# Router and expert projections of a routed attention layer in one unrolled block

## The chip, the cores and the metric

The program runs on one core of a Trainium2 chip. Its time is the device time of that core in microseconds (us): from the first to the last instruction, with a little around them. Five engines work in parallel, each through its own list of instructions in order: TensorE (PE, matrix products; PEld are its weight loads), VectorE (DVE), ScalarE (ACT), GpSimd (POOL) and SyncE (SP, which here only issues DMAs). They wait for one another by semaphores. DMAs are issued from SP, ACT or POOL and run on 16 shared DMA engines.

## The reference

A stack of four layers over 2048 tokens of 128 channels. The change touches one sublayer, the routed attention of layer 2 (`l2f_` in names):

```python
h = relu(layer_norm(x @ rW1.T + rb1, eps=1e-5) * ln_g + ln_b)
probs = softmax(h @ rW2.T + rb2)                  # 8 experts
tp, ti = top_k(probs, 2); tp = tp / tp.sum()
for e in range(8):                                # each expert is an attention with weights of its own
    q, k, v = heads(x @ qW[e].T + qb[e]), heads(x @ kW[e].T + kb[e]), heads(x @ vW[e].T + vb[e])
    out += ((softmax(q @ k.T * scale) @ v) @ oW[e].T + ob[e]) * gate[e]
```

Here x is the normalised input; there are 16 heads of 8 channels. Keys and values are needed of all tokens for all experts, queries only of the tokens that chose the expert.

## The kernel before

The sublayer `l2_ffn` has four stages, each a block (all engines meet at a block's end):

- `l2_router` (L2046): normalises the tokens (`NormBlock`: DVE statistics, PE transposes, ACT copies to `channels_n`), makes the hidden layer (PE L2118, DVE L2179 to L2189), logits (PE L2129), top 2 (DVE), each token's slot in a list sorted by expert (DVE L2214 to L2246), and adds the output bias (PE L2147). It also fills constants: POOL sets `v_and_ones` to one, and SP copies rows of ones into the two buffers of `k_parts` (L255, four DMAs of 96 KB that end in 3 partitions each).
- `l2_prepare` (L2252): a hardware loop of four rounds with two experts in each. Per expert, PE transposes four weight matrices (L2360), projects keys for all tokens into four PSUM banks (L161) and values in two halves (L2367, L2427). Keys are kept as three bf16 parts: ACT writes part hi (L2400), DVE the rest (L2422), ACT part mid (L2402), DVE part lo (L2431). SP stores everything in DRAM: `expert_w_out_dram`, `expert_w_q_dram`, `expert_v_dram` (L2312), then six DMAs of `l2f_k_parts_dram` (L281). Part buffers are double (`part_`, `other_`), the buffer of values is single, and so SP's stores of values must land before DVE writes the next (`v_stored`). SP also loads the weights (L2293) and biases (L2298 to L2302) of the expert after next, behind the stores of this one in its queue; the biases of keys and queries come as columns, 4 bytes to a partition. Beside it POOL scatters 32 times 128 token numbers into `query_list_dram` (L2344), loads two lines of that list (L2019) and gathers the tokens of the first two query tiles (L2023).
- `attention_loop` (starts with DVE L994) and `l2_collect`: not touched.

The order in each engine is as written; nothing reorders it.

Of the kernel before, what the change touches and what calls it, by code (L numbers as in the profile page):

```python
# [22 lines left out]
F32 = mybir.dt.float32  # L23
# [207 lines left out]
class AttentionConstants:  # L231
# [17 lines left out]
    def sync(self, sp):  # L249
        self.wait(sp)  # L250
        at = self.at
        ones = at.ones[:, :].unsqueeze(1).to_broadcast([3, NPAIR, T])
        for k in range(self.buffers):
            for j in range(2):
                sp.dma_start(at.kx[64 * j + ROWS:64 * j + ROWS + 3, k, :, :], ones).then_inc(self.ones_set, 16)  # L255
# [18 lines left out]


def store_keys(at, eng, e, parts, parts_ready, count, parts_stored):
    eng.wait_ge(parts_ready, count)
    for which, part in enumerate(parts):
        n = len(range(NR)[ROWS_OF_K[which]])
        for j in range(2):  # L280
            eng.dma_start(at.k_dram[bass.ds(e, 1), j, :, :, ROWS_OF_K[which], :].rearrange("e p d n t -> (e p d) n t"),  # L281
                          part[64 * j:64 * j + 64, :].unsqueeze(1).to_broadcast([64, n, T])).then_inc(parts_stored, 16)
# [1744 lines left out]
def l2_ffn(c, at, ins, fixed):  # L2027

    c.layer = "l2f_"
    E, K = 8, 2
    with ExitStack() as ctx:
        rt = Routed(c, ctx, E, K)
        gate = c.sb(ctx, "gate", [P, K, NT], F32)
        slot = c.sb(ctx, "slot", [P, K, NT], mybir.dt.uint32)
        row = c.sb(ctx, "row", [P, NT], mybir.dt.uint32)
        y_row = c.sb(ctx, "y_row", [P, K, NT], mybir.dt.uint32)
        l2_router(c, ins, rt, E, K, gate, slot, row, y_row, fixed)  # L2040
        l2_prepare(c, at, ins, rt, slot, row)
        attention_loop(c, at, 3, routed=rt)
        l2_collect(c, rt, gate, y_row)


def l2_router(c, ins, rt, E, K, gate, slot, row, y_row, fixed):  # L2046

    nc, ps = c.nc, c.ps
    W = P // 2
    with ExitStack() as ctx:  # L2050
# [4 lines left out]
        h, hh = c.sb(ctx, "hidden", [P, NT, W], F32), c.sb(ctx, "hidden_squared", [P, NT, W], F32)  # L2055
        hT = c.sb(ctx, "hiddenT", [W, T], F32)
# [6 lines left out]
        counts, offset = c.sb(ctx, "tile_counts", [P, NT, E], F32), c.sb(ctx, "tile_offset", [P, NT, E], F32)  # L2063
        more, tiles_of = c.sb(ctx, "more", [P, E, NT], F32), c.sb(ctx, "tiles_of", [P, E], F32)
        first, end, index = c.sb(ctx, "first_tile", [P, E], F32), c.sb(ctx, "end_tile", [P, E], F32), c.sb(ctx, "partition", [P, 1], F32)
# [3 lines left out]
        mixT = c.sb(ctx, "mixT", [E, T], F32)  # L2069
        norm = NormBlock(c)  # L2070
        (w_loaded, drawn, chain, wT_psum, wT_ready, h_psum, hvar_ready, hstd_ready, h_ready, hT_psum, hT_ready, lg_psum, shifted, exp_ready,
         sel_ready, rank_psum, mix_ready, mixT_psum, mixT_ready, ranked, of_tile_ready, of_tile_psum, ob_psum) = (c.sem("r_" + n) for n in (
             "w_loaded", "drawn", "chain", "wT_psum", "wT_ready", "h_psum", "hvar_ready", "hstd_ready", "h_ready", "hT_psum", "hT_ready",
             "lg_psum", "shifted", "exp_ready", "sel_ready", "rank_psum", "mix_ready", "mixT_psum", "mixT_ready", "ranked", "of_tile_ready",
             "of_tile_psum", "ob_psum"))
        loads = [(w1[:, :], ins["L2_ffn_rW1"]), (w2[:, :], ins["L2_ffn_rW2"]), (ob[:, :], ins["L2_ffn_ob"]),
                 (b1[:, :], row_view(ins["L2_ffn_rb1"], W)), (g1[:, :], column(ins["L2_ffn_ln_g"])),
                 (g0[:, :], column(ins["L2_ffn_ln_b"])), (b2[:, :], row_view(ins["L2_ffn_rb2"], E))]
# [8 lines left out]
        with nc.Block() as block:  # L2087
            @block.sync
            def _(sp):
                for dst, src in loads:  # L2090
                    sp.dma_start(dst, src).then_inc(w_loaded, 16)
                fixed.sync(sp)
                fixed.sync_end(sp)

            @block.gpsimd
            def _(pool):
                draw_order(c, pool, order, E, drawn)
# [3 lines left out]
                nc.gpsimd.memset(before[:, :], 1.0).then_inc(drawn, 1)  # L2101
                pool.wait_ge(drawn, DRAWN - 1)
# [3 lines left out]
                fixed.gpsimd()  # L2106
                fixed.wait(pool)

            @block.tensor
            def _(pe):  # L2110
                pe.wait_ge(w_loaded, 16 * len(loads))
                nc.tensor.transpose(ps[:, 4, 0:W], w1[:, :], c.ident[0:W, 0:W])
                nc.tensor.transpose(ps[0:W, 4, W:W + E], w2[:, :], c.ident[0:E, 0:E]).then_inc(wT_psum, 1)
                norm.tensor(pe)
                pe.wait_ge(wT_ready, 2)
                pe.wait_ge(norm.nT_ready, NC)
                for t in range(NT):
                    ins_ = nc.tensor.matmul(ps[:, 4 + t // 8, (t % 8) * W:(t % 8 + 1) * W], c.nT[:, t * P:(t + 1) * P], w1T[:, :],  # L2118
                                            start=True, stop=True)
                    if t % 8 == 7:  # L2120
                        ins_.then_inc(h_psum, 1)
                pe.wait_ge(h_ready, 1)
                for t in range(NT):
                    ins_ = nc.tensor.transpose(ps[0:W, t // 4, (t % 4) * P:(t % 4 + 1) * P], h[:, t, :], c.ident[:, :])
                    if t % 4 == 3:
                        ins_.then_inc(hT_psum, 1)
                pe.wait_ge(hT_ready, NC)
                for t in range(NT):
                    last = nc.tensor.matmul(ps[:, 6, t * E:(t + 1) * E], hT[:, t * P:(t + 1) * P], w2T[:, :], start=True, stop=True)  # L2129
                last.then_inc(lg_psum, 1)  # L2130
                pe.wait_ge(drawn, DRAWN)
                pe.wait_ge(sel_ready, 1)
                chosen = sel[:, :, :].rearrange("p t e -> p (t e)")
                nc.tensor.matmul(ps[:, 7, 0:P], before[:, :], chosen, start=True, stop=True)
                nc.tensor.matmul(ps[:, 7, P:2 * P], ones[:, :], chosen, start=True, stop=True)
                nc.tensor.matmul(ps[:, 7, 2 * P:2 * P + 1], before[:, :], ones[:, 0:1], start=True, stop=True).then_inc(rank_psum, 1)
                pe.wait_ge(mix_ready, 1)
                for t in range(NT):
                    ins_ = nc.tensor.transpose(ps[0:E, t // 4, (t % 4) * P:(t % 4 + 1) * P], mix[:, t, :], c.ident[:, :])
                    if t % 4 == 3:  # L2140
                        ins_.then_inc(mixT_psum, 1)
                pe.wait_ge(of_tile_ready, 1)
                nc.tensor.transpose(ps[0:1, 6, 0:P], of_tile[:, :], c.ident[:, :]).then_inc(of_tile_psum, 1)
                pe.wait_ge(mixT_ready, NC)
# [674 lines left out]
```

## Time and profile before

| | us |
|---|---|
| median of three runs | 3931.2 (3928.16 to 3935.24) |
| the profiled execution | 3919.58 |
| its span, first to last instruction | 3917.9 |
| `l2_router` in it | 1998.6 to 2067.6 |
| `l2_prepare` in it | 2068.0 to 2278.2 |
| attention of the sublayer starts | 2278.2 |

Times in the rows below are us from the start of the span. In a timeline row the first number is the start, the second the duration; "x" is the number of instructions merged; in brackets is the idle time before and what ended it. In a row of stretches, each engine has its busy time and its number of instructions; PEclk is the granted clock of TensorE (1.00 is 2.4 GHz, 0.50 is 1.2 GHz), then come the busy share of the DMA engines and the GB/s moved.

### The profile page before, as it was taken

The page shows a single profiled execution, that of the slowest core. Times are in us where ns is not written, and L with a number is a line of the kernel's source. Part 1 is how long each engine was busy: PE and PEld are TensorE (multiplying, and loading weights), DVE is VectorE, ACT ScalarE, POOL GpSimd, SP SyncE. Part 2 cuts the span into 40 slices and gives each one's busy share as a digit, 9 for nine tenths or more (in the row PEclk, how much of TensorE's full clock was granted, in tenths as well). Part 3 has the DMA queues.
Part 4 walks back from the last instruction along what each step waited for, and adds up shares of the span by engine and source line. Part 5 has one row for each costly group of instructions (what it writes and reads, how often), then busy time and mean ns, then how long its engine had stood idle before and what let it go on. Part 6 is the DMA issues. An engine that isn't in the chain of part 4 may idle for free. (4 is left out here: it accounts for less than half of the span.)

```text
span 3917.9 us, 127868 instructions
## 1 busy us (share of the span) xinstructions
PE 3201.4 (82%) x54200; PEld 2084.5 (53%) x54200; DVE 2926.3 (75%) x3610; ACT 2528.6 (65%) x4873; POOL 601.5 (15%) x1574
## 2 busy tenths in 40 slices
PE   2999999479998897565764449999999999999638
PEld 1666666335555674122433326666666666666424
DVE  5999999458884113898353359999999999999653
ACT  1899999447777333432211229999999999999622
POOL 0010000011100000464004011111111111111220
PEclk7999999779999898899866769999999999999859
DMA  5000000310000000540008755555454545455410
GB/s 117 9 8 9 7 10 5 84 34 11 9 7 3 22 16 9 173 144 31 5 5 129 234 152 123 130 124 134 117 135 117 135 116 135 117 135 117 108 32 11
DMA packets 198682, 295.81 MB, mean 76 GB/s; under 512 B 93668, under 2 KB 128042, under 8 KB 197062
## 3 DMA queue, kind: packets, MB, share of 16 engines
q1 hardware_dynamic: 191478, 276.38, 28.3%
q10 hardware_dynamic: 2048, 6.29, 0.9%
q8 instruction: 423, 6.93, 0.8%
q0 software_dynamic: 4592, 5.05, 0.6%
q14 instruction: 141, 1.16, 0.1%
HBM read 225.51 MB, written 53.39 MB: 71 GB/s over the span
## 5 line engine op out<-in xcount | busy, mean ns | idle before, releaser
L890 ACT ACTIVATE channels_qk<-psum 128x512 f32<-128x512 f32 x3842 | 2061.1, 595 | 263.7 <-PE psum L716 189.6
L958 DVE TENSOR_REDUCE l2f_chunk_max<-psum 128x2 f32<-128x1024 f32 x1144 | 1324.8, 1217 | 76.3 <-PE psum L691 67.8
L958 DVE TENSOR_REDUCE chunk_max<-psum 128x2 f32<-128x1024 f32 (+2 forms) x832 | 916.8, 1156 | 112.2 <-PE psum L691 62.6
L691 PE MATMUL psum<-l2f_k_parts,l2f_q_parts 48*128 48x512 bf16 x2288 | 697.0, 388 | 42.5 <-DVE l2f_chunk_max L958 31.2
L737 PE MATMUL psum<-channels_qk,l2f_v_and_ones 128*9 128x128 f32 x17920 | 698.5, 274 | 14.1 <-issue 14.1
L716 PE MATMUL psum<-l2f_q_parts,l2f_k_parts 51*128 51x128 bf16 x8968 | 706.5, 218 | 0.4 <-ACT l2f_minus_max_rows L938 0.4
L691 PE MATMUL psum<-k_parts,q_parts 48*128 48x512 bf16 (+3 forms) x1664 | 424.5, 382 | 103.2 <-DMA q_parts<-q_rows_dram 73.6
L716 PEld LDWEIGHTS psum<-l2f_q_parts,l2f_k_parts 51*128 51x128 bf16 x8968 | 482.4, 94 | 30.7 <-ACT channels_qk L890 23.2
L737 PE MATMUL psum<-channels_qk,v_and_ones 128*9 128x128 f32 x12544 | 492.7, 275 | 0.6 <-ACT channels_qk L890 0.5
L716 PE MATMUL psum<-q_parts,k_parts 51*128 51x128 bf16 x6272 | 432.5, 218 | 31.1 <-DMA q_parts<-minus_max_rows 10.5
L737 PEld LDWEIGHTS psum<-channels_qk,l2f_v_and_ones 128*9 128x9 f32 x17920 | 386.0, 90 | 121.3 <-issue 23.7
L691 PEld LDWEIGHTS psum<-l2f_k_parts,l2f_q_parts 48*128 48x128 bf16 x2288 | 208.5, 94 | 296.0 <-issue 157.5
L716 PEld LDWEIGHTS psum<-q_parts,k_parts 51*128 51x128 bf16 x6272 | 288.4, 94 | 93.8 <-ACT channels_qk L890 56.2
L737 PEld LDWEIGHTS psum<-channels_qk,v_and_ones 128*9 128x9 f32 x12544 | 271.0, 90 | 77.6 <-issue 11.2
L691 PEld LDWEIGHTS psum<-k_parts,q_parts 48*128 48x128 bf16 x1664 | 122.3, 94 | 288.0 <-issue 145.6
L1714 PE MATMUL psum<-l1a_state_c,identity 128*128 128x512 f32 x256 | 125.7, 616 | 89.4 <-DVE l1a_state_c L1699 89.4
L1413 DVE SCALAR_TENSOR_TENSOR x_normalised<-psum,l0f_expert_weights,x_normalised 128x128 f32<-128x128 f32 x128 | 36.0, 344 | 196.4 <-PE psum L1377 196.4
L609 POOL TENSOR_TENSOR l2f_minus_max_parts<-l2f_minus_max,l2f_one 128x4 bf16<-128x4 f32 x143 | 28.4, 199 | 916.6 <-DVE l2f_minus_max L965 916.6
L1665 ACT ACTIVATE psum<-l1a_delta,l1a_a 128x1024 f32<-128x1024 f32 x64 | 71.5, 1118 | 147.0 <-DVE l1a_input L1694 147.0
L1398 ACT ACTIVATE l0f_hidden<-psum,l0f_b_now 128x512 f32<-128x512 f32 x128 | 87.9, 687 | 118.2 <-PE psum L1368 118.2
L609 POOL TENSOR_TENSOR minus_max_parts<-minus_max,one 128x4 bf16<-128x4 f32 x128 | 25.5, 199 | 902.3 <-DVE minus_max L965 902.3
L1714 PEld LDWEIGHTS psum<-l1a_state_c,identity 128*128 128x128 f32 x256 | 43.9, 189 | 171.2 <-DVE l1a_state_c L1699 137.4
(476 smaller groups left out, 3178.0 us busy)
## 6 DMA issues: line engine op xcount, KB each, us to landing
l2f_k_parts<-l2f_k_parts_dram SPq DMA_DIRECT2D x588, 192.0 KB, 3.8
l2f_v_and_ones<-expert_v_dram SPq DMA_DIRECT2D x144, 288.0 KB, 4.3
l1a_bc_rows<-ssm_rows_dram SPq DMA_DIRECT2D x32, 512.0 KB, 4.7
expert_v_dram<-l2f_v_and_ones SPq DMA_DIRECT2D x8, 1152.0 KB, 4.3
channels_qk<-ssm_rows_dram SPq DMA_DIRECT2D x16, 512.0 KB
l2f_q_parts<-l2f_gathered_q_parts SPq DMA_DIRECT2D x444, 16.0 KB
k_parts<-k_rows_dram ACTq DMA_DIRECT2D x32, 192.0 KB, 7.6
q_parts<-q_rows_dram SPq DMA_DIRECT2D x64, 96.0 KB, 2.5
```

Of the source, the lines that this page charges most:

```text
L609: return g_.tensor_tensor(dst, src, ones.to_broadcast(list(src.shape)), ALU.mult)
L691: last = nc.tensor.matmul(c.ps[:, 2 * (n % 2) + j, 0:width], at.q[64 * j:64 * j + ROWS, tile % SLOTS, pair, :], kx(tile)[64 * j:64 * j + R ...
L716: last = nc.tensor.matmul(c.ps[:, ring.bank(i, place[j]), (2 * kk + pp) * P:(2 * kk + pp + 1) * P], kx(i)[64 * j:64 * j + ROWS + 3, pair, ...
L737: last = nc.tensor.matmul(oT[32 * m:32 * m + HD + 1, g * P:(g + 1) * P], vx(i)[:, kt, 4 * g + m, :], at.prob[:, s % 4, j, kk, pp * P:(pp + ...
L890: nc.scalar.activation(at.prob[:, s % 4, j, 0:kts, :].rearrange("p k q -> p (k q)"), c.ps[:, ring.bank(i, n), 0:kts * 2 * P], ACT.Exp, sca ...
L958: v.tensor_reduce(at.mx[:, 4 * g + 2 * pp:4 * g + 2 * pp + 2, chunk], c.ps[:, 2 * (n % 2):2 * (n % 2) + 2, 0:span.width(tile, chunk)], X, ...
L1398: nc.scalar.activation(mid[:, k % 2, f, :], ps[:, f, :], ACT.Gelu, bias=bnow[:, k // NC, f:f + 1]).then_inc(gelu_done, 1)
L1413: last = v.scalar_tensor_tensor(c.n[:, tile, :], ps[:, 4 + k % 2, t * P:(t + 1) * P], mix[:, tile, bass.ds(r * 2 + e, 1)], c.n[:, tile, :] ...
L1665: nc.scalar.activation(decay(step), delta[:, h, tokens(step)], ACT.Exp, scale=a[:, h, n:n + 1]).then_inc(da_ready, 1)
L1714: last = nc.tensor.matmul(ps[:, 2 * (step % 2) + b, :], c.ident[:, :], hc[:, step % U, b * 512:(b + 1) * 512], start=False, stop=step % S ...
```

## The change

`l2_router` and `l2_prepare` become one function, `l2_front`, with one block and no loop. Its parts:

- All weights are loaded at its start: expert 0's by four DMAs, the other seven's by four DMAs of 7 x 64 KB, into the second buffer of `k_parts`, which is free until the attention; all value biases by one DMA. Biases of keys and queries come as rows (two DMAs of 8 x 128), are reordered by ACT and transposed by PE.
- The router's loads are issued from ACT, not SP.
- The values have both buffers of `v_and_ones`, in quarters over two PSUM banks.
- Each engine's list holds an expert's steps and the router's in turn; the router's PSUM is bank 7 alone, so its transposes and logits take turns with ACT bank by bank.
- POOL makes part lo of experts 0 to 3, DVE of 4 to 7. The scatter on POOL comes after these, when DVE has the slots.
- The ones of `k_parts`' second buffer are placed at the end, when the weights there are no longer read.

```diff
             @block.sync
             def _(sp):
-                for dst, src in loads:
-                    sp.dma_start(dst, src).then_inc(w_loaded, 16)
-                fixed.sync(sp)
+                for n, m in enumerate("qkvo"):
+                    sp.dma_start(w[:, 0, n, :], ins[f"L2_ffn_{m}W"][0]).then_inc(w_loaded, 16)
...
+                    sp.dma_start(w[:, 1:E, n, :], ins[f"L2_ffn_{m}W"][1:E].rearrange("e p d -> p e d")).then_inc(all_w_loaded, 16)
...
+                fixed.place(sp, 0)
+                sp.wait_ge(norm.n_ready, NC)
+                sp.dma_start(rt.n_dram[:, :].rearrange("(t p) d -> p t d", p=P), c.n[:, :, :]).then_inc(n_stored, 16)
+                sp.wait_ge(rw_ready, 4)
+                for e in range(E):
+                    store_expert(e)
+                sp.wait_ge(o_stored, 32 * E)
+                fixed.place(sp, 1)
                 fixed.sync_end(sp)
...
+                def store_expert(e):
+                    sp.wait_ge(hi_ready, 4 * e + 4)
+                    store_part(e, 0)
+                    sp.wait_ge(wT_ready, 3 * e + 3)
+                    sp.dma_start(rt.w_out_dram[e], wT[:, e, 2, :]).then_inc(o_stored, 16)
+                    sp.dma_start(rt.w_q_dram[e], w_q[:, e, :]).then_inc(o_stored, 16)
+                    sp.wait_ge(v_ready, QUARTERS * (e + 1))
...
+                    sp.wait_ge(mid_ready, e + 1)
+                    store_part(e, 1)
+                    sp.wait_ge(lo_ready, e + 1)
+                    store_part(e, 2)
...
             @block.gpsimd
...
+                for e in range(E // 2):
+                    pool.wait_ge(rest_ready, 4 * e + 4)
+                    pool.wait_ge(mid_ready, e + 1)
+                    nc.gpsimd.tensor_tensor(parts[e % 2][2][:, :], rest, parts[e % 2][1][:, :], ALU.subtract).then_inc(lo_ready, 1)
                 pool.wait_ge(scattered, 16)
+                pool.wait_ge(slots_ready, 1)
...
             @block.scalar
+                def keys_hi(e):
+                    if e >= 2:
+                        act.wait_ge(parts_stored[e % 2], 96 * (e // 2))
                     for n in range(NC):
-                        act.wait_ge(k_psum, e * 4 + (n + 1))
+                        act.wait_ge(k_psum, 4 * e + n + 1)
...
             @block.vector
+                def values(e, quarters):
+                    if e >= 2:
+                        dve.wait_ge(v_stored[e % 2], 16 * (e // 2))
...
+                keys_rest(3)
...
+                link(v.tensor_copy(ranks[:, :], ps[:, 7, 0:2 * P + 1]))
+                values(3, range(QUARTERS))
...
+                keys_rest(4)
...
+                v.memset(many[:, 0:1], float(rt.least // 2)).then_inc(slots_ready, 1)
```

**PE**, from the normalised tokens on. Before, the router's products stand alone, and the loop with the experts' begins behind a branch; `l2f_w_qkvo` are the weights.

```order
L153 MATMUL psum<-identity,x_normalised 128x128 x16
L2118 MATMUL psum<-l2f_rw1T,channels_n 128x64 x16
L2124 MATMUL psum<-identity,l2f_hidden 64x128 x16
L2129 MATMUL psum<-l2f_rw2T,l2f_hiddenT 128x8 x16
L2134 MATMUL psum<-l2f_selected,l2f_before 128x128
```

Now (`l2f_k_parts` is the buffer in which the weights and their transposes lie, `channels_qk` the one in which the hidden layer lies):

```order
L153 MATMUL psum<-identity,x_normalised 128x128 x16
L2192 MATMUL psum<-identity,l2f_k_parts 128x128 x4
L161 MATMUL psum<-channels_n,l2f_k_parts 128x512 x4
L2214 MATMUL psum<-l2f_rw1T,channels_n 128x64 x16
L2207 MATMUL psum<-l2f_k_parts,channels_n 128x128 x16
L2192 MATMUL psum<-identity,l2f_k_parts 128x128 x4
L161 MATMUL psum<-channels_n,l2f_k_parts 128x512 x4
L2221 MATMUL psum<-identity,channels_qk 64x128 x16
L2207 MATMUL psum<-l2f_k_parts,channels_n 128x128 x16
L2192 MATMUL psum<-identity,l2f_k_parts 128x128 x4
L2265 MATMUL psum<-l2f_rw2T,channels_qk 128x8 x16
L161 MATMUL psum<-channels_n,l2f_k_parts 128x512 x4
```

The keys of expert 0 now stand ahead of the hidden layer, and the logits (L2265) behind the values of expert 1.

**SP**, one expert's steps. Before, the row of six key stores (L281, the first of them shown) stands between loads of weights ahead and of biases behind; ISA rows are waits on counts that a register holds.

```order
L2293 DMA l2f_w_qkvo<-in_L_ffn_oW_dram 128x128
L2308 ISA
L2308 DMA expert_w_out_dram<-l2f_wT_qkvo 128x128
L2309 ISA
L2310 ISA
L2310 DMA expert_w_q_dram<-l2f_w_and_b_q 128x129
L2311 ISA
L2312 ISA
L2312 DMA expert_v_dram<-l2f_v_and_ones 128x2304
L281 ISA
L281 DMA l2f_k_parts_dram<-l2f_part_hi 64x3x2048
```

Now, from the last loads to the first step of expert 1:

```order
L2127 DMA l2f_k_parts<-in_L_ffn_vb_dram 128x1024
L257 DMA l2f_k_parts<-l2f_ones_rows 3x8x2048 x2
L2131 DMA normalised_tokens_dram<-x_normalised 128x16x128
L2104 DMA l2f_k_parts_dram<-l2f_part_hi 64x3x2048 x2
L2111 DMA expert_w_out_dram<-l2f_k_parts 128x128
L2112 DMA expert_w_q_dram<-l2f_w_and_b_q 128x129
L2114 DMA expert_v_dram<-l2f_v_and_ones 128x2304
L2104 DMA l2f_k_parts_dram<-l2f_part_mid 64x2x2048 x2
L2104 DMA l2f_k_parts_dram<-l2f_part_lo 64x2048 x2
L2104 DMA l2f_k_parts_dram<-l2f_other_hi 64x3x2048 x2
```

No load stands between two experts' stores any more, and part hi goes out ahead of the values.

## Rows read from the trace of the kernel before

**Rows 1.** Stretches: the two blocks. Start:end, length, engines, PEclk, DMA share, GB/s.

```profile
1998.00:2068.00 70.00, 34.59 (x153) 29.80 (x153) 38.85 (x143) 11.39 (x19) 7.11 (x30) 0.52 0.04 7
2068.00:2278.00 210.00, 83.56 (x356) 60.60 (x356) 59.48 (x63) 40.81 (x67) 40.06 (x41) 0.67 0.83 194
```

**Rows 2.** Timeline: last copy to channels_n; first instruction of prepare; first of attention.

```profile
2012.43 0.60 ACT L177 ACTIVATE channels_n<-psum 128x512 f32<-128x512 f32 x1 [0.43 <-PE psum L153]
...
2068.03 0.33 SPq L2293 DMA_DIRECT2D l2f_w_qkvo<-in_L_ffn_qW_dram  x1
...
2278.18 0.48 DVE L994 MEMSET psum<- 128x512 f32 x1 [27.05 <-PEq L2280]
```

**Rows 3.** Waits, 2066 to 2300: waiter and releaser, us in total, times, longest.

```profile
ACT l2f_part_hi L2400 <- DMA l2f_w_and_b_q<-in_L_ffn_qb_dram: 68.4, 3, 37.5
...
ACT l2f_other_hi L2400 <- DMA l2f_w_and_b_q<-in_L_ffn_qb_dram: 39.9, 4, 15.0
...
DVE l2f_v_and_ones L2427 <- DMA expert_v_dram<-l2f_v_and_ones: 33.6, 6, 17.2
```

**Rows 4.** Timeline of SP: stores of values, experts 5 and 6.

```profile
2216.64 0.33 SPq L2312 DMA_DIRECT2D expert_v_dram<-l2f_v_and_ones  x1
...
2238.17 0.33 SPq L2312 DMA_DIRECT2D expert_v_dram<-l2f_v_and_ones  x1
```

**Rows 5.** DMA issues, 1980 to 2330: KB each, us from issue to landing.

```profile
expert_v_dram<-l2f_v_and_ones SPq DMA_DIRECT2D x8, 1152.0 KB, 4.3
l2f_k_parts_dram<-l2f_part_hi SPq DMA_DIRECT2D x8, 768.0 KB, 10.0
```

**Rows 6.** Stretches: ones placed; two under the scatter; one expert's stores; the first load.

```profile
2008.00:2024.00 16.00, 11.25 (x48) 9.76 (x48) 7.43 (x19) 2.39 (x4) 0.00 (x0) 0.50 0.15 24
2100.00:2110.00 10.00, 0.18 (x1) 0.18 (x2) 1.23 (x1) 0.00 (x0) 7.60 (x8) 0.50 1.05 79
...
2120.00:2130.00 10.00, 0.00 (x0) 0.00 (x0) 0.00 (x0) 0.00 (x0) 0.00 (x0) 0.62 1.05 98
2238.00:2254.00 16.00, 4.90 (x20) 4.20 (x20) 5.76 (x5) 2.61 (x5) 0.00 (x0) 0.50 0.92 275
...
4.00:6.00 2.00, 0.00 (x0) 0.00 (x0) 0.00 (x0) 0.00 (x0) 0.00 (x0) 1.00 1.04 323
```

**Rows 7.** Timeline of PE: keys of an expert; half of its values at either clock.

```profile
2084.90 3.60 PE L161 MATMUL psum<-channels_n,l2f_wT_qkvo 128*128 128x512 f32 x8
...
2088.33 1.95 PE L2367 MATMUL psum<-l2f_wT_qkvo,channels_n 128*128 128x128 f32 x16
...
2243.89 3.78 PE L2367 MATMUL psum<-l2f_wT_qkvo,channels_n 128*128 128x128 f32 x16 [4.64 <-DVE l2f_v_and_ones L2427]
```

**Rows 8.** Groups by line in the router, 1998 to 2068: busy, mean ns, idle before.

```profile
L2118 PE MATMUL psum<-l2f_rw1T,channels_n 128*128 128x64 f32 x32 | 7.1, 422 | 0.8 <-ACT channels_n L177 0.8
L2129 PE MATMUL psum<-l2f_rw2T,l2f_hiddenT 64*128 64x8 f32 x32 | 7.0, 358 | 0.9 <-ACT l2f_hiddenT L2163 0.9
...
L2124 PE MATMUL psum<-identity,l2f_hidden 128*64 128x128 f32 x16 | 3.6, 421 | 8.2 <-DVE l2f_hidden L2189 8.2
```

**Rows 9.** Timeline of DVE in the router: first and last of the slots' chain.

```profile
2048.37 0.07 DVE L2216 MEMSET l2f_tile_offset<- 128x8 f32 x1
...
2059.05 0.17 DVE L2246 TENSOR_SCALAR l2f_y_row<-l2f_where 128x16 uint32<-128x16 f32 x1
```

**Rows 10.** Timeline of POOL: first scatter; list loaded; tokens gathered.

```profile
2074.05 1.05 POOL L2344 DMA_INDIRECT query_list_dram<-l2f_row,l2f_slot  x1 [3.16 <-DMA query_list_dram<-l2f_blank_list]
...
2135.60 1.17 POOL L2019 DMA_DIRECT2D l2f_gathered_index<-query_list_dram  x2 [17.69 <-DMA query_list_dram<-l2f_row,l2f_slot]
...
2144.56 0.97 POOL L2023 DMA_INDIRECT l2f_gathered_tokens<-normalised_tokens_dram,l2f_gathered_index  x1 [0.31 <-issue]
```

**Rows 11.** DMA queue of POOL in 2090 to 2100 and in 2120 to 2130: packets, MB, share.

```profile
q0 software_dynamic: 53, 0.00, 0.4%
...
q0 software_dynamic: 242, 0.00, 5.1%
```

More of the change, by code:

```diff
@@ L2079, in l2_router @@
+        ROUTER_LOADS = 16 * len(router_loads)
         DRAWN = E + NT + 3
@@ L2105, in _ @@
                                         pattern=[[1, P]], channel_multiplier=-1).then_inc(drawn, 1)
[L2106 to L2144, printed above, removed]
-                pe.wait_ge(ranked, 1)
-                for t in range(NT):
-                    ins_ = nc.tensor.matmul(ps[:, 4 + t // 4, (t % 4) * P:(t % 4 + 1) * P], mixT[:, t * P:(t + 1) * P], ob[:, :],
-                                            start=True, stop=True)
-                    if t % 4 == 3:
-                        ins_.then_inc(ob_psum, 1)
@@ new lines, in _ @@
+                turn_weights(0)
+                pe.wait_ge(rw_loaded, ROUTER_LOADS)
+                nc.tensor.transpose(ps[:, 7, 0:W], w1[:, :], c.ident[0:W, 0:W])
+                nc.tensor.transpose(ps[0:W, 7, W:W + E], w2[:, :], c.ident[0:E, 0:E])
+                pe.wait_ge(b_ordered, 2)
+                for n in range(2):
+                    last = nc.tensor.transpose(ps[:, 7, P + n * E:P + (n + 1) * E], b_order[:, n, :], c.ident[0:E, 0:E])
+                last.then_inc(rw_psum, 1)
+                norm.tensor(pe)
@@ new lines, in _ @@
+                turn_weights(1)
+                pe.wait_ge(norm.nT_ready, NC)
+                project_keys(0)
+                pe.wait_ge(rw_ready, 4)
+                project_hidden(0)
+                pe.wait_ge(h_added, 1)
+                project_hidden(1)
+                project_values(0, range(QUARTERS))
+                turn_weights(2)
+                project_keys(1)
+                pe.wait_ge(h_ready, 1)
+                for k in range(NC):
+                    turn_hidden(k)
+                project_values(1, range(QUARTERS))
@@ new lines, in _ @@
+                turn_weights(3)
+                pe.wait_ge(hT_ready, NC)
+                for t in range(NT):
+                    last = nc.tensor.matmul(ps[:, 7, t * E:(t + 1) * E], hT[:, t * P:(t + 1) * P], w2T[:, :], start=True, stop=True)
+                last.then_inc(lg_psum, 1)
+                project_keys(2)
+                project_values(2, range(QUARTERS))
+                turn_weights(4)
+                project_keys(3)
+                pe.wait_ge(drawn, DRAWN)
+                pe.wait_ge(sel_ready, 1)
@@ new lines, in _ @@
+                evacuate(c, act, 0, c.nT, norm.nT_psum, 0, norm.nT_ready)
+                copy_weights(1)
+                act.wait_ge(rw_ready, 4)
+                keys_hi(0)
+                keys_mid(0)
+                act.wait_ge(hvar_ready, 1)
+                nc.scalar.activation(total[:, :], total[:, :], ACT.Sqrt).then_inc(hstd_ready, 1)
+                copy_weights(2)
+                keys_hi(1)
+                for k in range(NC):
+                    act.wait_ge(hT_psum, k + 1)
+                    nc.scalar.activation(hT[:, k * 512:(k + 1) * 512], ps[0:W, 7, :], ACT.Relu, bias=g0[:, :], scale=g1[:, :]).then_inc(hT_ready, 1)
@@ L2409, in _ @@
+                for k in range(NC):
+                    act.wait_ge(mixT_psum, k + 1)
+                    nc.scalar.activation(mixT[:, k * 512:(k + 1) * 512], ps[0:E, 7, :], ACT.Copy).then_inc(mixT_ready, 1)
+                keys_mid(5)
+                copy_weights(7)
+                for e in (6, 7):
+                    keys_hi(e)
+                    keys_mid(e)
             @block.vector
@@ L2411, in _ @@
                 v = nc.vector
[L2412 to L2418 removed]
+                link = Chain(dve, chain)
@@ L2436, in l2_collect @@
+                keys_rest(7)
+                values(7, range(QUARTERS))
+                keys_lo(7)
 def l2_collect(c, rt, gate, y_row):
```

504 lines of the change are left out of this document (265 added, 239 removed).

## The prediction

> **What bounds the kernel now.** The change touches two blocks, so I read the stretches of these first, then the marks of their ends, then who waits in them, and last the DMA queues. The two blocks take from 1998.6 to 2278.2, 280 us of the 3917.9 [rows 1, 2]. In the first, the DMA engines are busy 4% of the time, and neither PE (34.6 us of 70) nor DVE (38.9) is full: the router is one dependent chain. In the second they are busy 83% of 210 us and move 194 GB/s, while PE has 83.6 us of work, DVE 59.5, ACT 40.8 [rows 1]. So the second block is the DMA queue's: it waits for data only a sixth of its time, the first leaves it idle.
>
> Two things keep the queue from doing better. First, a loop between stores and loads: the biases of expert e+2 are issued behind the stores of e, and ACT, which opens an expert's keys, waited 68.4 + 39.9 us for them; DVE waited 33.6 us for the single buffer of values [rows 3]. From one store of values to the next it takes 21.5 us [rows 4], of which the queue is full for 16, from 2238 to 2254 [rows 6]. Second, the scatter. It began at 2074 and had landed at 2135.6 [rows 10]. Under it the queue shows a share of 1.05 and yet moves 79 and 98 GB/s; without it, 275 [rows 6].
>
> **What must be moved.** Per expert 1152 KB of values [rows 5], keys of 2 x 768 KB for part hi [rows 5], and in the same shape (3, 2 and 1 rows of the six) 2 x 512 and 2 x 256 for mid and lo, with some 128 KB of weights: 4352 KB or 4.46 MB. At 275 GB/s that is 16.2 us, for eight experts 130 us. The change moves the same.
>
> **The change, part by part.**
>
> *Loads first.* 2.1 MB of weights, 0.5 MB of value biases: the nearest row is the load of the kernel's start, 323 GB/s [rows 6], so 8 us; twice that if pieces of 512 bytes in seven experts at once go slower. It lies beside the normalisation, which ends at 2013.0 [rows 2], and costs nothing at either end. The column loads of biases and the weight loads between stores go: with them goes the wait of rows 3.
>
> *Keys of expert 0 ahead of the router.* From 2013.0, PE transposes and projects, ACT copies, DVE makes the rest: I put the first store at 2021 (transposes and their copies 2, keys 6, all at the low clock). The store of normalised tokens, 1 MB, goes ahead of it and is done by then.
>
> *Experts 0 to 3 and the router in one order.* PE per expert: keys 3.6 us at clock 1.00 [rows 7], 7.2 at 0.50; values 2 x 1.95 or 2 x 3.78 [rows 7]; transposes about 1. That is 8 or 16 us. Between them stand hidden layer 7.1, its transposes 3.6, logits 7.0 [rows 8] and the small products for the ranks, say 1.5, all at the low clock. To the values of expert 3 this is 4 x 16 + 19 = 83 us at the low clock and about 42 at the high; PE also waits for DVE's layer norm of the hidden layer (8.2 us before [rows 8], part of it now under values; I take 6) and, bank 7 being one, four times for ACT between transposes (4 us). So the values of expert 3 are ready at 2013 + 93 = 2106 on a low clock. On a high one the queue leads instead: 2021 + 4 x 16.2 = 2086. PE granted 0.67 over the old block [rows 1] and will be fuller here: I take the middle, 2096. Values, mid and lo of expert 3 then need another 10 us: half the stores are out at **2106** (2096 to 2115). The queue has gaps in this part, because part hi goes out early and then SP stands at `v_ready` until DVE has worked off the router's piece ahead of the values; behind it in SP's list are mid and lo, and nothing else waits for them as the buffers are double.
>
> *The scatter.* It needs DVE's slots: behind the values of expert 3 stand the chain of slots, 10.8 us from L2216 to L2246 [rows 9], and the rest of expert 4, 3 us of DVE's 7.4 per expert (59.5 over 8, [rows 1]), less a count of about 1 us that is put off. So it starts at 2096 + 12.5, about 2109. POOL's own part lo of experts 0 to 3 is long done. It took 61.5 us before [rows 10]; I take that. With it go 61.5 x 0.088 = 5.4 MB of stores, at the mean of 79 and 98 GB/s [rows 6]. It ends at 2170; list and gather end 10 us later [rows 10] and are hidden by the stores.
>
> *Stores of experts 4 to 7.* 17.8 MB from 2106 on: 0.8 until 2109, 5.4 under the scatter, 11.6 behind it at 275 GB/s, 42 us: to 2212. The compute of an expert (PE at most 16 us; DVE 7.4 and ACT 5.1, an eighth of rows 1) hides under 16.2 us of stores, with double buffers. The old scatter phase had other small transfers in it; if the queue does better there, this term falls by up to 15 us, and if large stores hold the scatter up to 80 us it grows by 12.
>
> *Ones at the end.* Two of the four copies of ones are now behind the last store. The four took 16 us at 24 GB/s, 2008 to 2024 [rows 6], as they end in three partitions; two take **8 us**, uncovered.
>
> *The attention* begins at 2212 + 8 = 2220 instead of 2278.2: **58 us** earlier; one block boundary less gives half a us. Nothing behind it changes.
>
> The sum: 3919.6 - 59 = 3860.6 for an execution like the profiled one. The median of the runs shown lies 11.6 above that execution, so I predict 3931.2 - 59 = **3872**. Ends of the terms, fast clock and quick scatter: 2096 + 3 + 50, 5.1 MB moved under it, 11.9 MB at 299 GB/s (275 over its share 0.92) to 2189, + 8 = 2197, gain 81. Slow: 2115 + 3 + 75, 10.4 MB left, 38, + 8 = 2239, gain 39.
>
> A rule of the skill bears on the scatter's term. The row shows the scatter's queue at 5.1% of the engines [rows 11] while the stores fall to a third. The Trainium skill, DMA: Bandwidth & Descriptors, Queues, rings and completion order, says that each engine takes turns between queues packet by packet; a packet of 4 bytes should then cost a store packet almost nothing. By that rule the stores would run on at 260 under the scatter; it is rival A. The same page, Specifications, says that writes under 512 bytes are read-modify-write, which speaks for the row.
>
> **Rivals.**
>
> A. *The scatter was not what slowed the queue.* The stretch 2080 to 2130 also held column loads, and its share is over 1 with little moved; what slowed it may go with the change. Then all 17.8 MB run at 275 GB/s from 2106: 65 us, to 2171, + 8 = 2179: gain 99, **3832**. For it: the small share [rows 11]. Against: the columns came with every expert, and the stretches with them but without a scatter are fast [rows 6].
>
> B. *The experts run in lockstep all the same.* Engines take their lists in order; if each expert's chain (copy, rest, mid, lo, then the stores) lies open as before, each costs 21.5 us [rows 4], and hidden layer and logits, 14 us of PE [rows 8], lie open between the first four. Half the stores are then out at 2021 + 86 + 14 = 2121; 3 + 61.5 us of scatter bring 1.4 experts, the other 2.6 take 56, and 8: to 2249, gain 29, **3902**. For it: PE at the low clock needs 16 us an expert, no less than the stores. Against: the bias loads that closed the loop are gone. That the order on paper does nothing, because the router's pieces wait for one another anyway, ends in the same place.
>
> C. *Slower than before: the scatter starves.* In 2090 to 2100 it got 53 packets, against 242 in 2120 to 2130 [rows 11], while POOL issued at the same pace. At the mean of the two, 148, its 61.5 us hold about 910. If large stores hold it at 53 per 10 us throughout, it lasts 171 us from 2109, and list and gather follow: 2290, so that the attention starts 12 us late, **3943**. It decides from a scatter of 159 us on. Against: with large key stores beside it (2120 to 2130) it ran at its best pace.
>
> **How the numbers follow.** My case (gain 39 to 81) 0.64; A (81 to 105) 0.15; B (5 to 39) 0.16; C 0.03; no change 0.02. The range leaves out about half of A and most of B and all of C: gain 36 to 91, so 3840 to 3895. A measurement of this kernel can tell about 0.2%, 8 us, from no change. Faster by more: 0.64 + 0.15 + 0.15 = 0.94; within 0.02 + 0.01; slower 0.03.
>
> **What the profile of the changed kernel would show.** The first key store at 2020 to 2025 (loads and early keys). Waits of ACT's keys on a DMA of biases gone; in their place waits of ACT for its part buffer in experts 4 to 7, when the queue leads. Stores of values of experts 0 to 3 spaced by 17 to 21 us with a queue that is not full; a scatter starting at 2105 to 2115 and lasting 50 to 75 us with 80 to 100 GB/s beside it; 16 us an expert at a full queue behind it; and 8 us of 24 GB/s at the very end. It would be wrong if the scatter let the stores pass (A), if the queue kept gaps after 2170 (B), or if the gather ended the block (C). Outside the block times must stay as they are.

## The result, and the profile after

The changed kernel takes 3840.1 us (median of 4 runs, 3830.1 to 3844.4), the kernel before 3930.6 (3928.2 to 3935.2): a ratio of 0.976, with an interval of 0.975 to 0.978. That is 90 us less where 59 were forecast: the median lies on the range's lower end, and the ratio on the 3931.2 us that the forecast started from gives 3838, below it. The profiled execution took 3844.4 with a span of 3842.6, its block of router and experts 198.4 us (1994.52 to 2192.94) where the two blocks had 279.6 [rows 2].

The first fence is SP's timeline of the block (start, length, instruction), the second POOL's, the third DVE's: first load; first store of keys; values and the last keys of expert 3; the last step before the values of expert 5 and these; the last keys of expert 7; the ones; first scatter and the load of the finished list; the attention's first instruction.

```profile
1994.52 0.33 SPq L2122 DMA_DIRECT2D l2f_k_parts<-in_L_ffn_qW_dram  x1
...
2013.58 2.76 SPq L2104 DMA_DIRECT2D l2f_k_parts_dram<-l2f_part_hi  x2
...
2082.22 1.72 SPq L2114 DMA_DIRECT2D expert_v_dram<-l2f_v_and_ones  x1
...
2086.09 4.92 SPq L2104 DMA_DIRECT2D l2f_k_parts_dram<-l2f_other_lo  x2
...
2110.57 0.45 SPq L2112 DMA_DIRECT2D expert_w_q_dram<-l2f_w_and_b_q  x1
2142.34 0.33 SPq L2114 DMA_DIRECT2D expert_v_dram<-l2f_v_and_ones  x1
...
2177.04 4.92 SPq L2104 DMA_DIRECT2D l2f_k_parts_dram<-l2f_other_lo  x2
2182.00 2.14 SPq L257 DMA_DIRECT2D l2f_k_parts<-l2f_ones_rows  x2
```

```profile
2091.67 2.43 POOL L2170 DMA_INDIRECT query_list_dram<-l2f_row,l2f_slot  x1 [12.77 <-DVE l2f_many L2479]
...
2147.66 1.17 POOL L2012 DMA_DIRECT2D l2f_gathered_index<-query_list_dram  x2 [13.04 <-DMA query_list_dram<-l2f_row,l2f_slot]
```

```profile
2192.94 0.48 DVE L987 MEMSET psum<- 128x512 f32 x1 [24.82 <-PEq L2098]
```

The stretches of the same profile (start:end, length, PE's granted clock, the DMA engines' busy share, GB/s):

```profile
2020.00:2030.00 10.00, 0.52 0.39 93
2030.00:2040.00 10.00, 0.82 0.91 286
...
2060.00:2070.00 10.00, 0.66 0.51 149
2070.00:2080.00 10.00, 1.00 0.98 277
...
2090.00:2100.00 10.00, 0.66 0.93 256
2100.00:2110.00 10.00, 0.74 1.02 118
...
2130.00:2140.00 10.00, 0.50 0.86 80
...
2150.00:2160.00 10.00, 1.00 0.94 275
2160.00:2170.00 10.00, 0.98 0.94 299
...
2186.00:2188.00 2.00, 0.50 0.18 25
```

They show four parts: from 2013 to 2091 a queue that is full but for two holes (2020, 2060); the scatter, with 118 to 126 GB/s beside it in 2100 to 2130 and 80 in 2130 to 2140; a full queue at 275 to 299; and at the end 25 GB/s of ones. Under the scatter SP also stands at `v_ready` for 31 us (2110.57 to 2142.34), as the values of expert 5 come late; what this does to the block is taken up with the runs without a scatter. The wait of ACT's keys for bias loads [rows 3] is gone. What PE's first pieces cost now, from its timeline (keys of expert 0, hidden layer, logits):

```profile
2008.99 3.78 PE L161 MATMUL psum<-channels_n,l2f_k_parts 128*128 128x512 f32 x8
2012.61 1.89 PE L2214 MATMUL psum<-l2f_rw1T,channels_n 128*128 128x64 f32 x16
2015.35 3.10 PE L2214 MATMUL psum<-l2f_rw1T,channels_n 128*128 128x64 f32 x16 [0.85 <-DVE channels_qk L2400]
...
2045.11 3.73 PE L2265 MATMUL psum<-l2f_rw2T,channels_qk 64*128 64x8 f32 x32
```

Hidden layer (1.9 + 3.1) and logits (3.7) took 8.7 us where they took 14.1 [rows 8]: PE was granted 0.78 in 2013.6 to 2091.0 instead of 0.52 in the old router [rows 1].

### The profile page after: what moved, and what is told of

It is laid out like the page before. It is cut to its first block and busy times, and to the rows that moved or that the text cites. A ratio compares the mean times of both kernels' runs of the same rounds, so it can differ in the third digit from the quotient of the medians.

```text
span 3842.6 us, 127345 instructions
## 1 busy us (share of the span) xinstructions
PE 3198.5 (83%) x54198; PEld 2078.6 (54%) x54198; DVE 2924.8 (76%) x3614; ACT 2528.8 (66%) x4874; POOL 616.8 (16%) x1578
## 5 line engine op out<-in xcount | busy, mean ns | idle before, releaser
L951 DVE TENSOR_REDUCE chunk_max<-psum 128x2 f32<-128x1024 f32 (+2 forms) x832 | 916.5, 1153 | 109.2 <-PE psum L684 61.5
```

The costliest lines, as they stand in the source:

```text
L951: v.tensor_reduce(at.mx[:, 4 * g + 2 * pp:4 * g + 2 * pp + 2, chunk], c.ps[:, 2 * (n % 2):2 * (n % 2) + 2, 0:span.width(tile, chunk)], X, ...
```

## Experiments

The block is counted from the first load to the attention's first instruction, the rest from there to the end of the span. Block and rest are each from one profile of the kernel, times are medians of several executions; "beside" is the kernel before in the same comparison. The same kernel's block differed by up to 11 us between profiles, so smaller differences of block say little. Chips A and B are two chips on which the comparisons ran; the kernel before takes 3930 us on A and 3907 to 3910 on B.

| kernel | chip | block | rest | time | beside | ratio (interval) |
|---|---|---|---|---|---|---|
| before_again | B | 280.7 | 1642 | 3919.6 (one execution) | 3910.5 | |
| before_third | A | 290.5 | 1650 | 3928.5 | 3930.3 | 1.000 (0.998 to 1.001) |
| after_again | B | 192.5 | 1649 | 3835.5 | 3906.5 | 0.981 (0.979 to 0.983) |
| after_third | A | 195.4 | 1650 | 3841.9 | 3930.3 | 0.977 (0.975 to 0.979) |
| before_unrolled | B | 273.8 | 1642 | 3909.9 | 3910.5 | 1.000 (0.999 to 1.001) |
| router_first | A | 248.6 | 1651 | 3892.7 | 3932.7 | 0.990 (0.988 to 0.992) |
| one_v_buffer | A | 201.7 | 1650 | 3842.7 | 3930.3 | 0.977 (0.975 to 0.979) |
| before_no_scatter | A | 255.2 | 1651 | 3894.5 | 3932.7 | 0.990 (0.988 to 0.992) |
| after_no_scatter | A | 171.3 | 1653 | 3812.7 | 3932.7 | 0.970 (0.968 to 0.972) |
| half_scatter | A | 185.2 | 1653 | 3827.3 | 3930.3 | 0.974 (0.972 to 0.976) |
| scatter_paced | B | 232.2 | 1646 | 3869.8 | 3910.5 | 0.989 (0.988 to 0.991) |
| ones_by_row | A | 196.2 | 1655 | 3840.5 | 3932.7 | 0.976 (0.974 to 0.978) |
| ones_early | B | 198.3 | 1643 | 3840.1 | 3910.5 | 0.981 (0.980 to 0.983) |
| ones_in_attention | B | 195.1 | 1650 | 3833.5 | 3906.5 | 0.982 (0.980 to 0.983) |
| parts_first | B | 198.0 | 1640 | 3825.5 | 3906.5 | 0.979 (0.978 to 0.981) |
| both | B | 188.5 | 1653 | 3827.4 | 3906.5 | 0.980 (0.978 to 0.982) |

### What the scatter costs

*after_no_scatter*, *before_no_scatter*: POOL's loop of 32 scatters and the wait for them are out.

```
-                for t in range(NT):
-                    for k in range(K):
-                        nc.gpsimd.indirect_dma_start(out=rt.list_dram...)
-                pool.wait_ge(scattered, 16 * (1 + K * NT))
```

> The changed kernel with the 32 scatters of the list left out; the list stays zero, so every slot names row 0 and the output is another, with the same amount of work behind it. Theory S (the scatter takes the engines' time from the stores): 8.3 MB moved in its 56 us would need 30 us at 275 GB/s, so the block ends 26 us earlier (attention 172 us after the block's start instead of 198) and the time is about 3814; the stalls of PE and DVE in 2100 to 2140, which no data explains, are gone. Rival D (the stores were slow there because their data came late, SP standing at v_ready from 2110.6 to 2142.3): within 8 us of 3840, the same stalls.

> The kernel before with the 32 scatters left out (same remark on the list). Theory S: 61.5 us at 88 instead of 275 GB/s cost 42 us, of which the loop between loads and stores (21.5 us an expert, eight of them 172 of the 210 us) leaves 38 to be seen: 3892. Rival A of the prediction (the scatter is innocent): 3930, and the stretches around 100 us after the block's start still move 80 to 100 GB/s.

3812.7 and 3894.5 where theory S had 3814 and 3892. The block of the changed kernel is 24 to 27 us shorter, that of before 35 on the same chip (290.5 to 255.2). In the stretches of after_no_scatter the place is filled:

```profile
2090.00:2100.00 10.00, 0.82 0.95 297
2100.00:2110.00 10.00, 0.70 0.94 260
```

So the scatter takes the stores' time, and rival A falls: a queue with under a tenth of the share takes over half of the other's bytes. Two ways are open for it: the stores that are queued go slower, or the values come late (SP at `v_ready`) so that fewer are queued. Rival D had the late values as a cause of their own; they are not, since without the scatter SP's 31 us there shrink to at most 4.2. The slower stores alone can cost as much: in after_again (chip B) SP's longest wait for values is 8.2 us, the engines do not stop, the DMA share stays above 1 from 2100 to 2150, and the block is about as long (192.5). From its stretches:

```profile
2110.00:2120.00 10.00, 0.82 1.11 149
...
2140.00:2150.00 10.00, 0.50 1.07 153
```

The rule of turns by packets (the Trainium skill, DMA: Bandwidth & Descriptors, Queues, rings and completion order) does not tell this loss; the measurement decides.

*scatter_paced*: four semaphores in turn, each scatter waits for the fourth before it. *half_scatter*: `for k in range(1)`, the second choice's rows are not scattered.

```
+                        n = K * t + k
+                        if n >= 4:
+                            pool.wait_ge(paced[n % 4], 16 * (n // 4))
```

> The changed kernel with at most 4 scatters on their way at a time instead of about 10. Theory F (a long row of scatter packets in each engine's queue holds up stores and fetches of code): the stops of 5 to 17 us shrink, SP gets its values of expert 5 earlier than 2142, 5 to 10 us gained: 3832. Rival G (each scattered word costs an engine its time, however they are spread): the scatter lasts as long or longer, and the time stays within 4 us of 3840.

> The changed kernel with 16 of the 32 scatters (the second choice's are left out, so the list is incomplete and the output another). Theory T (the stores lose by the time in which a scatter is under way, some 0.45 to 0.55 of their rate): it lasts about 30 us instead of 56 to 60, and the block is 12 to 15 us shorter. Rival N (it is the number of words, each 0.1 us of an engine): the same here, but it would have made scatter_paced cost nothing; only a cost that does not halve (under 6 or over 20 us) speaks against both.

Pacing made it worse, by 34 to 40 us of block; neither F nor G had that. The scatter lasted from 2088.1 to 2213.8. POOL's wait, and two stretches:

```profile
POOL query_list_dram L2174 <- DMA query_list_dram<-l2f_row,l2f_slot: 83.9, 23, 9.5
```

```profile
2130.00:2140.00 10.00, 0.50 0.97 129
2140.00:2150.00 10.00, 0.84 1.13 170
```

In 2100 to 2160 the stores got 129 to 170 GB/s, with four scatters on their way at most. Half the scatters lasted 39 us (2078.8 to 2118.2), not the 30 expected, and cost 14 us of block over none, where all 32 cost 24 in 55.6 us: 0.35 and 0.43 us for each us under way. The paced kernel's block is 61 us longer than without a scatter, but this is not all the stores' loss. From 2210 to 2218 the DMA engines are idle (share 0.00 to 0.01): stores and ones are through at about 2210, 219 us into the block and some 48 us later than the whole block without a scatter, which is 0.39 for each of 122 us. The last 13 us are the scatter's own end, the list and the gather, the path that rival C of the prediction had. The loss goes by time, roughly, and not by the number of words, since the paced kernel scatters as many as the others. The way to make it cheaper is to make it shorter.

### What each part of the change brings

*router_first*: PE, ACT and DVE do the whole router ahead of expert 0; all else as in the changed kernel. PE's list:

```
-                project_keys(0)
                 pe.wait_ge(rw_ready, 4)
                 project_hidden(0)
...
                 for q in range(QUARTERS):
                     add_out_bias(q)
-                    project_values(6, (q,))
...
+                for e in range(E):
+                    project_keys(e)
+                    project_values(e, range(QUARTERS))
```

> The changed kernel with the interleave alone undone: on PE, ACT and DVE all steps of the router stand ahead of all steps of the experts; loads, bias rows, double buffer and unrolled code stay. Theory I (the interleave is worth the time in which the queue stood idle): first key store about 70 us after the block's start instead of 19, then 130 us of stores, 30 us for the scatter, 8 of ones: attention at 238 instead of 198, time about 3880. Rival L (most of the gain is the loop of loads that went; the router's steps only push the experts' steps back when mixed with them, PE being slow): at most 15 us lost, 3855.

The order is worth 53 us of block and 52 of time, more than I had put down: the first store of keys comes at 2073.44, 86 us into the block, and until then the queue stands:

```profile
2030.00:2040.00 10.00, 0.50 0.00 1
```

Part of this is where the scatter stands. DVE has the slots at 2049.82, while the queue is idle, but POOL's list still has the scatter behind part lo of expert 3, so that it starts at 2117.92, beside the stores. A router ahead of the experts with its scatter in the idle stretch was not run; how much of the 53 us it would save is open.

*before_unrolled*: Python loops for `eng.Fori`. *one_v_buffer*: values of all experts go through `at.v[:, 0]`, and DVE waits for the store of those before.

```
-                with eng.Fori(0, E // 2) as r:
+                for r in range(E // 2):
```

```
-                    if e >= 2:
-                        dve.wait_ge(v_stored[e % 2], 16 * (e // 2))
+                    if e >= 1:
+                        dve.wait_ge(v_stored[(e - 1) % 2], 16 * ((e - 1) // 2 + 1))
```

> The kernel before with the loop over the experts written out, nothing else changed. Theory U (unrolling as such brings no time, the gain is in the order and the loads, and costs a little where the scatter runs: code that is not in a loop is fetched by DMA, and the fetches wait behind the scatter, which is what stopped PE, DVE and ACT in 2105 to 2140 of the changed kernel): 3930 to 3945, with waits of DVE or PE of 5 to 17 us for nothing in the trace while the scatter runs. Rival V (the stops come from something else in the changed kernel): no such waits, 3925 to 3932.

> The changed kernel with one buffer of values instead of two: the values of expert e+1 wait until the store of those of e has landed, some 7 us after its issue. Theory B (the double buffer matters little, since part hi of the next expert is stored meanwhile and the old 33.6 us of waits were mostly the scatter's): under 8 us slower than after_third. Rival M (values and stores then run in lockstep, some 4 us for each of eight experts): 30 us slower.

Unrolling brings nothing (1.000; its one profile has a block 7 us shorter than before_again's), the second buffer 1 us of time (6 of block, in one profile each). router_first is still 40 us faster than before. The loads that left the queue are the likely cause, as the experts no longer take 21.5 us each [rows 4], but this is argued by exclusion and not shown: no run puts them back, and part lo on POOL, the biases as rows and part hi ahead of the values were not tried alone either.

### The end of the block

*ones_by_row*: each copy of ones in three, one partition each, in 16 pieces. *ones_early*: the two copies ahead of mid and lo of expert 7. *ones_in_attention*: behind the loads of tile 0, PE waits before tile 1.

```
+            for r in range(3):
+                sp.dma_start(self.at.kx[row:row + 1, k, :, :].rearrange("p a (b t) -> p (a b) t", b=2), ...)
```

```
-                fixed.place(sp, 1)
-                fixed.sync_end(sp)
...
+                routed.fixed.place(sp, 1)
                 for g in range(G - 1):
                     load_group(1, g, second)
```

> The changed kernel with every copy of ones split in three, one partition each in 16 pieces of 2 KB, so that 16 DMA engines share it instead of 3. Theory E (the last 8 to 10 us are three engines' work): the end term falls to 2 us, time about 3833. Rival P (the six receiving partitions set the rate): the same 8 to 10 us, 3840.

> The changed kernel with the last two copies of ones ahead of the stores of parts mid and lo of expert 7 instead of behind them. Theory H (the copies hold 3 of 16 engines, 0.18 of the queue's share, and the six receiving partitions set their pace): the stores run beside them and the 8 us shrink to 2 or 3: 3834. Rival Q (each engine works off its own row of packets, so that the three that carry ones are late with their part of the stores by the same 8 us): 3840.

> The changed kernel with the last two copies of ones issued in the attention's block, behind the loads of tile 0, and waited for by PE ahead of tile 1. Theory Y (the copies at the block's end are uncovered, 8 to 10 us): 8 to 10 us less than after_again. Rival Z (the first tiles' loads are the bound there and the copies push them back): within 3 us of after_again.

None brought time. By row, the copies keep all engines busy and move hardly more than the 25 GB/s of three engines (stretches of ones_by_row): the number of engines does not set the pace, as rival P has it. Whether the six partitions written or the three read do was not separated.

```profile
2176.00:2178.00 2.00, 0.50 0.99 31
2178.00:2180.00 2.00, 0.50 0.97 29
```

ones_early's block is as long as the changed kernel's, as rival Q has it. With the ones in the attention the time is 3833.5 against after_again's 3835.5, as rival Z has it. The attention gives back what it was spared: the ones stand ahead of loads in SP's list, the load of the row maxima is issued 48.3 us after the attention's start (2178.67) instead of 39.4 (after_again, start 2189.11), and PE waits for it. Ahead after_again, then ones_in_attention:

```profile
2234.04 0.69 PE L709 MATMUL psum<-l2f_q_parts,l2f_k_parts 51*128 51x128 bf16 x9 [2.33 <-issue]
```

```profile
2232.13 0.69 PE L712 MATMUL psum<-l2f_q_parts,l2f_k_parts 51*128 51x128 bf16 x9 [10.84 <-issue]
```

The block itself is not shorter in this profile (195.1 against 192.5), since its last keys were stored 7.6 us later than after_again's.

*parts_first*: SP stores mid and lo ahead of the values in experts 0 to 5; *both*: with the ones in the attention.

```
+                    if e >= 6:
+                        store_values()
                     sp.wait_ge(mid_ready, e + 1)
                     store_part(e, 1)
                     sp.wait_ge(lo_ready, e + 1)
                     store_part(e, 2)
+                    if e < 6:
+                        store_values()
```

> The changed kernel with the stores of parts mid and lo ahead of the store of values for experts 0 to 5. In the changed kernel SP stands at v_ready from 2021.2 to 2029.9 and from 2061.0 to 2068.0 while mid and lo (1.5 MB, 5.6 us of queue) of that expert are ready from 2020.5 and 2062.5. Theory W (the block is the sum of bytes over 275 GB/s plus the queue's idle stretches): about 10 us less, block 189. Rival X (what the queue gains in front it gives back at the scatter, or the values then come late and hold the double buffer): within 3 us of after_again.

> The two edits together: W and Y give 18 us less than after_again, X and Z nothing.

The hole closes (263 GB/s in 2020 to 2030 instead of 93), half of the stores are out 2 to 5 us sooner, but the block had 198.0 and 188.5 us against 192.5 to 198.4 without the edit. 3825.5 and 3827.4 against 3835.5 us: the ratio's intervals overlap with after_again's. A few us may be in it; it is not shown, and no version here surely beats the changed kernel.

### The same kernels again, on two chips

> The kernel before, unchanged, for a second profile. Four profiles of variants show 1650 to 1655 us from the start of the attention to the end of the program, the profile of before 1640. Theory J (the profiled execution of before was a fast one behind the block, by chance): about 1651 here and a span of 3929, with 280 us in the two blocks. Rival K (the new code slows the attention): 1640 again.

> The kernel before, unchanged, timed and profiled beside after_third on one chip. If the chips differ in the block of before, the two blocks are not 280 to 281 us here; if they differ in the attention, it takes more than 1642 us.

> The changed kernel, unchanged, beside the next three on one chip, and for a second profile. Block of 198 to 200 us again (84 of gain against the 281 of before); the stops of PE and DVE under the scatter (17.5 and 10.0 us in the first profile, none in the profile of ones_early, whose block had the same length) may or may not be there: if the block keeps its length without them, they cost nothing.

> The changed kernel, unchanged. Block 193 to 199 us, attention 1640 to 1655; the gain in time is that of the two blocks, 82 to 88 us, if nothing outside them differs, and 70 to 75 if the attention gives back some 10.

before_again was to tell whether the new code slows the attention (rival K) or the first profile of before was fast behind the block by chance (J, some 1651 us). It had 1642, which spoke for K; before_third, on A, then had 1650, like the changed kernel there, so on A the new code does not slow the attention. On B the changed kernel had 1649 and its variants 1640 to 1653, and there it is open.

On chip B the gain is 71 us, on A 88. In one profile each, the block of before differs, 280.7 and 290.5, the changed one's hardly (192.5, 195.4). The blocks alone would give 88 us on B and 95 on A; of the 17 and 7 us that are missing in the times, 6 on B lie behind the block (1642 and 1649), the others are not explained by these profiles. On A, before stands still under its scatter. From before_third, timelines of DVE and PE, and a stretch:

```profile
2084.79 1.22 DVE L2427 TENSOR_TENSOR l2f_v_and_ones<-psum,l2f_b_v 128x1024 f32<-128x1024 f32 x1 [18.44 <-issue]
2105.19 1.23 DVE L2427 TENSOR_TENSOR l2f_v_and_ones<-psum,l2f_b_v 128x1024 f32<-128x1024 f32 x1 [19.18 <-remote]
```

```profile
2086.07 3.78 PE L2367 MATMUL psum<-l2f_wT_qkvo,channels_n 128*128 128x128 f32 x16 [19.01 <-issue]
```

```profile
2080.00:2090.00 10.00, 0.50 0.02 0
```

The engines stop for 18 and 19 us while nothing that they need is late in the trace, the stores have nothing to send, and the first keys go out at 2108.78, 125 us into the block and after the scatter (2058.9 to 2106.2). In before_again they left at 2085.09, 90 us into it. The changed kernel has the same stops on A (after_third):

```profile
ACT l2f_k_parts L2303 <- remote: 24.7, 1, 24.7
DVE l2f_v_and_ones L2390 <- remote: 20.8, 3, 9.2
...
DVE l2f_other_lo L2382 <- issue: 9.3, 1, 9.3
```

after_again on B has none, and its block is as long; that half of the stores are out by then and what is queued and double buffered covers most of a stop would explain it, but was not tried.

## Why the prediction was right or wrong

**Direction and mechanism held.** The router was one chain beside an idle queue, its pieces between the stores were worth the most, the scatter slowed the stores, the ones stood uncovered at the end. The sizes did not hold, and the step that failed most is one term: what passes beside the scatter. Of the profile's shift of the attention within the block, 58 forecast and 81 measured, by the steps of the sum:

- *Loads and first key store.* Forecast 22.4 us into the block, 19.1 measured: transposes and keys ran at nearly the high clock (the keys took 3.78 us, I had put 6). 3 us.
- *Experts 0 to 3.* Half of the stores out at +107.5 forecast, +96.5 measured (2086.09 + 4.92), 11 us early with those 3. The mis-sized step here is PE's: I took the middle between a low and a high clock, with the router's pieces low throughout; they took 8.7 us instead of 14.1, the clock was 0.78. "On a high one the queue leads instead" is what came: 0.9 busy but for the two holes. The holes are as forecast, SP at `v_ready`.
- *The scatter's start*, +110.4 forecast, +97.2 measured: 11 of these 13 us are the same. The chain of slots took what was forecast (13.3 us behind the values of expert 3, 12.5 forecast); the scatter began 0.7 us behind the half of the stores instead of 3.
- *The scatter's length and what passes beside it.* 61.5 us and 5.4 MB forecast; 56.0 us and 8.0 MB (143 GB/s) measured. This is the largest error: 5.5 us of length and some 8 of bytes. I had taken the mean of two stretches of before, 79 and 98, and these were two of the three slowest. The whole of the old scatter moved 112 GB/s, or 6.9 MB, which was to be read from the same trace:

```profile
2074.05:2135.60 61.55, 0.69 1.00 112
```

  Here there were 118 to 126 in the middle, and in the first 8 us still 256. I had named the other small transfers of the old phase as a gain of up to 15 us, and put it in the range only; no run tells how much of the step from 112 to 143 they are.
- *Stores behind it.* 275 GB/s forecast, 275 to 299 measured: right.
- *Ones.* 8 us forecast, 11 measured with the wait for their landing and the change of block.

11 + 2 + 5.5 + 8 - 3 makes the 23 us that are missing, to half a us. The block's gain of 81 us is just the fast end that I had worked out (81), and inside the stated gains of 36 to 91. What put the time at the edge is the rest:

**The other 9 us are put down to the base, and not shown.** I subtracted from 3931.2, the median, a gain read from a profile that took 3919.6. The two were not the same: [rows 2] shows a block of 279.6 and a rest of 1640, as chip B's before_again (280.7 and 1642); the medians look like chip A's, where they are 290.5 and 1650. The gap of 11.6 us was to be seen, and I carried it along as a constant. If the two were of different chips, some 10 us more lay in the very blocks that the change replaces, and went with it. Which chip the first profile ran on is not known, and with one profile of before on A, and a part ahead of the blocks that took 1980 to 1999 us on either chip, 9 us can also be the spread between executions.

**The rivals.** A is refuted: without the scatter 27 us go. B (lockstep) did not happen: 15 to 16 us an expert at a full queue. C (the scatter starves) neither: 56 to 64 us, unless it is slowed on purpose, as in scatter_paced, where it did end the block. Of the signs asked for, the waits of ACT for its part buffer came in after_again (17.2 + 15.5 us) but not in the first profile, where the engines stop instead. The first key store came 3 us early in the block, the scatter 13; beside the scatter there was more than the 80 to 100 GB/s.

## What to carry to other kernels

Where a dependent chain leaves the DMA queue idle, put the stores' work between its steps: that was 52 us of some 90 here, against a router ahead of the experts with the scatter left where it was. Taking loads out of the store queue is the likely part of the rest; the loop's unrolling and the second buffer were worth next to nothing. A scatter of single words costs the other queue about half of its rate for as long as it is under way, so it should be dense and short, not spread. To price it, read a rate over the whole of such a phase, not from the slowest stretches. And a profile whose time lies off the median of the runs is not a base to subtract from until one knows in which stretch they differ: if it is in the part that changes, the gain may change with it.

## What the runs showed of the hardware

- A queue of single-word writes with 1 to 9% of the engines' share took 24 to 27 us of 56 from stores that run at 260 to 297 GB/s without it; paced so that it lasted 126 us, it took some 48 from them, and the block then waited 13 more for the scatter itself.
- Copies that end in six partitions run at 25 GB/s on three DMA engines and at 29 to 31 on sixteen, with these at a share of 0.97 to 0.99: more engines bring next to nothing.
- On one of two chips, engines stop for up to 27 us while a scatter runs, with the operands there and even with nearly idle DMA engines (before_third); on the other the longest such stop was 4.7 us (before_unrolled), and in the two kernels without a scatter, both run on the first chip, there is none. The cause is open. The Trainium skill, Runtime: NRT & Kernel Launch, Instruction fetch mechanics, says that the engines' code comes by DMA too, mostly hidden; a fetch that is late behind the scatter was the explanation that before_unrolled was to test, and it ran on the chip without stops. The traces speak against it: the code queues show no packet in 2078 to 2106 of before_third or in 2100 to 2142 of the changed kernel, though stops end in both stretches (2084.79 and 2105.19; 2118.77, 2131.83 and 2138.76).
- The part behind the block, which is the same code, took 1640 to 1655 us, most of it 1642 or 1650: more than most edits tried here brought.
